# Rotary embedding of a transformer block's projection: pairs in two channel tiles, products on VectorE, sums on GpSimd

## What is computed

```python
h = rmsnorm(x, g1) * (1 + scale1) + shift1
q, k, v = split(h @ w_qkv + b_qkv, 3)          # 16 heads of 32 channels
x0, x1 = q[..., 0::2], q[..., 1::2]            # the same for k
q = interleave(x0 * cos - x1 * sin, x1 * cos + x0 * sin)
attn = softmax(q @ k.T / sqrt(32)) @ v
```

## Time and profile before

| | before |
|---|---|
| median of 3 runs | 3583.11 us (3581.57 to 3583.68) |
| the profiled execution's own time | 3584.84 us |
| its span in the trace | 3583.0 us |
| busy: PE, DVE, ACT, POOL | 90%, 57%, 44%, 46% |
| `stage_a` in the trace | about 67 us to 438 us |
| one of its blocks in the steady part | 44.27 us |
| PE busy in that block, granted clock | 38.09 us, 0.92 of full speed |
| DVE, ACT, POOL busy in that block | 35.35, 17.45, 11.46 us |

### The profile page before, as it was taken

How to read it: one execution, slowest core, us unless ns; L and a number is a source line. 1 busy time by engine, 2 the same in 40 slices (tenths; PEclk the granted TensorE clock), 3 DMA queues, 4 the chain that set the end, 5 groups by cost and what they waited for, 6 DMA issues and landing times. The chain is left out here.

```text
span 3583.0 us, 53307 instructions
## 1 busy us (share of the span) xinstructions
PE 3218.5 (90%) x15180; PEld 2074.7 (58%) x15180; DVE 2025.6 (57%) x3254; ACT 1572.8 (44%) x2848; POOL 1665.3 (46%) x732
## 2 busy tenths in 40 slices
PE   5888789999999999999999994433999998999999
PEld 5666644444444444444444442432888886788887
DVE  2887677878777876878787783533322221322222
ACT  1333217676677766777676773233211111211111
POOL 0222318888788887888788886554100000100000
PEclk9999859999999999999999997766999999999999
DMA  4444449898898988899798987554411211411210
GB/s 168 141 141 142 134 91 194 179 195 189 165 196 183 194 176 171 181 188 199 160 194 178 193 191 166 170 182 161 144 47 47 94 47 49 143 66 47 94 47 24
DMA packets 179320, 508.04 MB, mean 142 GB/s; under 512 B 25914, under 2 KB 43434, under 8 KB 145966
## 3 DMA queue, kind: packets, MB, share of 16 engines
q0 software_dynamic: 36240, 248.53, 34.2%
q1 hardware_dynamic: 132308, 233.59, 21.7%
q10 hardware_dynamic: 10512, 22.81, 1.9%
HBM read 175.18 MB, written 93.62 MB: 75 GB/s over the span
## 5 line engine op out<-in xcount | busy, mean ns | idle before, releaser
L733 DVE TENSOR_REDUCE b_mpart<-b_m 128x1 f32<-128x512 f32 x2136 | 1325.9, 685 | 385.2 <-PE b_m L783 381.3
L672 ACT ACTIVATE b_pt<-b_s 128x512 f32<-128x512 f32 x2048 | 1115.0, 596 | 522.3 <-PE b_s L808 466.4
L711 POOL TENSOR_TENSOR b_acc<-b_acc,b_pt 128x2048 f32<-128x2048 f32 x225 | 1049.2, 4663 | 204.9 <-DMA b_pt<-b_pt 204.2
L808 PE MATMUL b_s<-b_qs,b_ks 98*128 98x512 f32 x2050 | 890.9, 435 | 23.7 <-ACT b_pt L672 23.7
L783 PE MATMUL b_m<-b_ks,b_qs 96*128 96x512 f32 x2136 | 787.2, 415 | 20.5 <-issue 20.2
L808 PEld LDWEIGHTS b_s<-b_qs,b_ks 98*128 98x128 f32 x2050 | 387.3, 189 | 675.3 <-ACT b_pt L672 617.5
L860 PE MATMUL b_o<-b_pt,b_vg 128*32 128x512 f32 x4096 | 549.5, 609 | 0.0
L783 PEld LDWEIGHTS b_m<-b_ks,b_qs 96*128 96x128 f32 x2136 | 417.6, 196 | 96.2 <-DVE b_mpart L733 26.3
L1245 DVE SCALAR_TENSOR_TENSOR d_uf<-d_a,keep_chan,d_sg 128x512 f32<-128x512 f32 x128 | 96.1, 751 | 578.1 <-PE d_a L1273 578.1
L1197 POOL DMA_DIRECT2D d_raw<-in_w_fc x32 | 24.0, 755 | 591.7 <-POOLq L1122 495.7
L1216 ACT ACTIVATE d_sg<-d_g,keep_chan 128x512 f32<-128x512 f32 x128 | 88.1, 689 | 419.7 <-PE d_g L1273 419.7
(11 more groups left out here) (130 smaller groups left out, 3606.6 us busy)
## 6 DMA issues: line engine op xcount, KB each, us to landing
b_pt<-b_pt POOLq DMA_DIRECT2D x225, 1024.0 KB, 8.1
b_ks<-scratch_qk_hi SPq DMA_DIRECT2D x36, 512.0 KB, 5.6
b_qs<-scratch_qk_hi SPq DMA_DIRECT2D x68, 256.0 KB, 5.5
scratch_qk_hi<-a_q_hi SPq DMA_DIRECT2D x64, 256.0 KB, 2.5
scratch_qk_lo<-a_q_lo SPq DMA_DIRECT2D x64, 256.0 KB, 2.8
d_h_hi<-scratch_h_hi SPq DMA_DIRECT2D x16, 1024.0 KB, 7.4
d_h_lo<-scratch_h_lo SPq DMA_DIRECT2D x16, 1024.0 KB, 9.6
d_y<-scratch_y SPq DMA_DIRECT2D x16, 1024.0 KB, 8.0
```

The costliest lines, as they stand in the source:

```text
L672: act.activation(pt[:, kt % RING, h, :], ps_s[:, i % LEAD, :], ACT.Exp, scale=SCALE).then_inc(p_ready, 1)
L711: pool.tensor_tensor(acc[slot][:], acc[slot][:], pt[:, (2 * n + 3) % RING, :, :], ALU.add).then_inc(pool_added, 1)
L733: dve.tensor_reduce(mpart[slot][:, i // 4, i % 4:i % 4 + 1], ps_m[:, i % EARLY, :], AX.X, ALU.max).then_inc(max_done, 1)
L808: pe.matmul(ps_s[:, i % LEAD, :], ks[kslot][0:QR, h, kt * P:(kt + 1) * P], qs[qslot][0:QR, h, :], start=True, stop=True).then_inc(st_done, 1)
```

## The change

The host lays the channels of q and k apart: of every 256 channels the even ones come first and the odd ones second, in weights and bias. Two neighbouring channel tiles are then one pair: tile 2p holds x0 and tile 2p+1 holds x1 of the same heads. The tables of cosine and sine have the same rows for both and no sign.

- VectorE makes four products for a pair with one instruction each, `scalar_tensor_tensor`, (PSUM + bias) x table, straight from `ps_qk`: x0 cos, x0 sin, x1 sin, x1 cos.
- GpSimd makes the two sums (`rotate`: a subtraction and an addition of products) into `yq`, and one pair later the two remainders (`split_lo`).
- ScalarE keeps the rounding (`round_q`) and loses the copy out of PSUM. The norm's `squares`, `roots` and `normalise` come behind the rounding of pairs 0, 1 and 2; `means` and `rstd` on VectorE come behind the products of pairs 1 and 2.
- TensorE waits for the products of the pair two before, in place of ScalarE's copies.
- SyncE stores `hi` of pair p and then `lo` of pair p-1. Each store is again 128 rows of 2 KB; in HBM a head's 16 even channels now stand ahead of its 16 odd ones.

```diff
+        prod = m.sb("prod", [P, 2, 4, TB])
+        yq = m.sb("yq", [P, 2, 2, TB])
 # SyncE
+                for p in range(NP):
+                    store("qk_hi", q_hi, hi_ready, 0, hi_stored, it, s, p)
+                    if p:
+                        store("qk_lo", q_lo, lo_ready, 4, lo_stored, it, s, p - 1)
+                store("qk_lo", q_lo, lo_ready, 4, lo_stored, it, s, NP - 1)
 # ScalarE
-                    act.activation(q[:, t % 2, :], ps_qk[:, t % 4, :], ACT.Identity,
-                                   bias=chan[:, C_BQK + t:C_BQK + t + 1]).then_inc(q_ready, 1)
+                for p in range(NP):
+                    round_q(blk, p)
                     if more:
-                        if t == 2:
+                        if p == 0:
                             squares(blk + 1)
-                        if t == 3:
+                        if p == 1:
                             roots(blk + 1)
-                        if t == 4:
+                        if p == 2:
                             normalise(blk + 1)
 # GpSimd
+            def rotate(blk, p):
+                pair = NP * blk + p
+                pool.wait_ge(prod_ready, 4 * pair + 4 + 8)
+                pool.wait_ge(lo_ready, 2 * pair + 2)
+                for half, op in enumerate((ALU.subtract, ALU.add)):
+                    pool.tensor_tensor(yq[:, p % 2, half, :], prod[:, p % 2, 2 * half, :], prod[:, p % 2, 2 * half + 1, :], op).then_inc(yq_ready, 1)
...
             def body(it, s, more):
+                blk = 2 * it + s
+                for p in range(NP):
+                    rotate(blk, p)
+                    if p:
+                        split_lo(blk, p - 1)
+                split_lo(blk, NP - 1)
 # VectorE
-                    dve.stream_shuffle(rot[:, t % 2, :], q[:, t % 2, :], swap).then_inc(shuf_done, 1)
+                    for half, table, to in ((0, cos, 0), (0, sin, 3), (1, sin, 1), (1, cos, 2)):
+                        t = 2 * p + half
+                        dve.wait_ge(qk_ps, 2 * pair + half + 1)
+                        dve.wait_ge(yq_ready, 2 * pair + 2)
+                        dve.nop(nofuse=True)
+                        dve.scalar_tensor_tensor(prod[:, p % 2, to, :], ps_qk[:, t % 4, :], chan[:, C_BQK + t:C_BQK + t + 1],
+                                                 table[:, now], ALU.add, ALU.mult).then_inc(prod_ready, 1)
                     if more:
-                        if t == 2:
+                        if p == 1:
                             means(blk + 1)
-                        if t == 3:
+                        if p == 2:
                             rstd(blk + 1)
 # TensorE
-                    pe.wait_ge(q_ready, NT * blk + t + 1)
+                    pe.wait_ge(prod_ready, 4 * (NP * blk + t // 2) + 4)
```

More of the change, by code:

```diff
@@ L237, in _ @@
             for i in range(2):
[L238 removed]
+                sp.sem_inc(hi_stored[i], 32)
+                sp.sem_inc(lo_stored[i], 32)
                 sp.sem_inc(v_stored[i], 16)
@@ L242, in _, with store @@
             sp.dma_start(x[:], xv[1, 0]).then_inc(x_in, 16)
+            def store(name, src, ready, credit, done, it, s, p):
+                pair = NP * (2 * it + s) + p
+                for half in range(2):
+                    sp.wait_ge(ready, 2 * pair + half + 1 + credit)
+                    sp.dma_start(qk_out[name][p // 2, s, p % 2, half, :, :, bass.ds(it * TB, TB)],
+                                 f32(src[:, p % 2, half, :])).then_inc(done[p % 2], 16)
             def body(it, s, more):
                 blk = 2 * it + s
[L246 to L251, removed]
+                for p in range(NP):
[3 more added lines that the diff above has]
+                store("qk_lo", q_lo, lo_ready, 4, lo_stored, it, s, NP - 1)
                 if more and not (isinstance(it, int) and s == 0):
@@ L321, in body, with round_q @@
                         round_h(blk + 1, 1 - s, c)
[L323 to L327, removed]
+            def round_q(blk, p):
+                pair = NP * blk + p
+                for half in range(2):
+                    act.wait_ge(yq_ready, 2 * pair + half + 1 + 4)
+                    act.wait_ge(hi_stored[p % 2], 32 * (NP // 2 * blk + p // 2 + 1))
+                    act.activation(q_hi[:, p % 2, half, :], yq[:, p % 2, half, :], ACT.Copy).then_inc(hi_ready, 1)
             run(act, body)
@@ L332, in _, with split_lo @@
         def _(pool):
-            pool.sem_inc(qc_ready, 2)
-            def body(it, s, more):
[L336 to L341, removed]
+            pool.sem_inc(yq_ready, 4)
+            pool.sem_inc(lo_ready, 4)
+            def rotate(blk, p):
+                pair = NP * blk + p
+                pool.wait_ge(prod_ready, 4 * pair + 4 + 8)
+                pool.wait_ge(lo_ready, 2 * pair + 2)
+                for half, op in enumerate((ALU.subtract, ALU.add)):
+                    pool.tensor_tensor(yq[:, p % 2, half, :], prod[:, p % 2, 2 * half, :], prod[:, p % 2, 2 * half + 1, :], op).then_inc(yq_ready, 1)
+            def split_lo(blk, p):
+                pair = NP * blk + p
+                for half in range(2):
+                    pool.wait_ge(hi_ready, 2 * pair + half + 1)
+                    pool.wait_ge(lo_stored[p % 2], 32 * (NP // 2 * blk + p // 2 + 1))
+                    pool.tensor_tensor(q_lo[:, p % 2, half, :], yq[:, p % 2, half, :], f32(q_hi[:, p % 2, half, :]),
+                                       ALU.subtract).then_inc(lo_ready, 1)
+            def body(it, s, more):
+                blk = 2 * it + s
[4 more added lines that the diff above has]
+                split_lo(blk, NP - 1)
             run(pool, body)
```

66 lines of the change are left out of this document (21 added, 45 removed).

## The result

The changed kernel takes 3562.75 us (median of 5 runs, 3560.96 to 3568.23) against 3583.11 us before, 20 us less. The ratio, taken over all runs of both, is 0.9949 with a 95% interval of 0.9937 to 0.9961, which is 14 to 23 us faster. The profiled execution took 3560.96 us, with a span of 3558.8 us, 24.2 us shorter than that of before.

A forecast was written before the change was run, and what follows sets the result against it. TensorE (90% busy) was taken as the bound, its projection pauses waiting for `hf` from a late VectorE. From 3583.0 us, 27 us for seven blocks and 5 us for the last were subtracted: 3551 us, range 3531 to 3574.

The forecast's parts named there:

- a full fall of the clock in each block: Projection blocks: TensorE drops to 1.2 GHz behind every pause, costing 2.7 us each; 41.8 us a block, 3561 us in all.
- The place of the pause and the products' price: Projection: TensorE's 6.16 us wait for `hf` goes, 3.8 us on `normalise` replaces it; products take 0.75 us with GpSimd busy.
- The rival that products and GpSimd exclude each other: Projection: each product waits for one GpSimd operation (1.25 + 0.75 us), a pair costs 8 us; 3596 us, chance 0.07.
- GpSimd at 1.25 us an operation: Projection: GpSimd's 16 added operations take 20 us a block, 5.0 us a pair against TensorE's 5.6, so it keeps up.
- VectorE near 20.5 us a block: Projection: VectorE loses 26.8 us of rotation, gains 12.0 us of products, falling from 35.35 to about 20.5 us a block.
- `rstd` held up by GpSimd: Projection, behind pair 2's products: four small operations each wait for one GpSimd operation, 4 x 1.24 us; `rstd` ready at 23.6.
- the race: `rstd`'s reciprocal and GpSimd's sums start within 0.1 us; rival with all four small operations unhindered: 3528 us, chance 0.13.
- The starved `means`: Projection: `means` gets in only at 18.0 us behind four GpSimd operations, transposes start at 28.2; 3574 us, chance 0.10.
- The clock behind the pause: Projection: a 3.8 us pause lies between 2.05 (full pace) and 4.56 (slowed); 0 to 2.7 us a block, middle 1.35 taken.
- The last block: Projection's last block, without `rstd`: last v store issued at 36.2 us from its start instead of 41.3, a gain of 5 us.
- I take nothing: SyncE's q and k stores: new HBM order bounded at nothing to 0.33 us more an issue; zero taken since 2 KB rows stay whole.
- The prediction's other remark: Other projection blocks: v stores queued behind the last remainder's store cost nothing, but would from a delay of about 2 us.

The follow-up runs named there:

- the copy: Changed kernel with ScalarE copying each q/k tile with bias to SBUF and VectorE multiplying from there, not from PSUM: 3572.38 us, ratio 0.9985 to the kernel before.
- the SyncE order alone: Changed kernel with eight instructions of satisfied waits (3544.54 us), plus next input's load and first two v stores issued ahead of last pair's lo stores: 3544.83 us.
- the first edits: Against 3544.54 us (changed kernel, eight added instructions): norm one pair earlier 3541.39; also ScalarE rounding h tiles 0, 1 before pair 3 3541.15; only SyncE's store order 3544.83.
- all three together: Changed kernel with eight added instructions (3544.54 us), plus earlier norm, ScalarE's earlier rounding of h tiles 0 and 1, and SyncE's new store order: 3516.41 us.

## Why the prediction came out as it did

The forecast was 3551 with a range of 3531 to 3574; the measured 3562.75 lies inside, 12 us above it. That it lies inside is in part luck: the projection stage gained more than forecast, and a stage that the sum left out lost more than that. It is also near the number that the prediction gave for a full fall of the clock in each block (3561). That is chance too: the clock fell in four blocks, and the missing time is elsewhere.

**The place of the pause and the products' price: right.** The argument was that TensorE waits for `hf` because VectorE is 11 us behind, that the products cost 0.75 us from PSUM, GpSimd busy or not, and that the wait for `hf` goes. Measured were 0.742 us and no such wait. The rival that products and GpSimd exclude each other (3596) is refuted for the PSUM source. From SBUF they do get in each other's way, as the copy showed: 0.93 to 0.98 us a product on average and up to 1.79, though not the 2.0 for each that the rival took.

**GpSimd at 1.25 us an operation: nearly.** Sums took 1.29 us and remainders 1.34 on average, 20.6 us a block for the 20 forecast. It kept up.

**VectorE near 20.5 us a block: too low.** It was 25.0 and 24.6. The sum left out the work that now meets a busy GpSimd: four `h_lo` at 0.97 us on average instead of 0.69 (1.1 us), and the small operations of the norm, 4.9 us a block instead of 1.9. With these 4.1 us it is 24.6. The schedule had the second term, the sum of VectorE's time had not. It is not what made the total wrong: TensorE's waits in these blocks end on `normalise`.

**`rstd` held up by GpSimd: right in kind, one step too many.** The forecast had all four small operations waiting, 1.24 us each. In the steady block the race went to VectorE for the first one:

```profile
220.66 0.16 DVE L68 TENSOR_TENSOR a_newton<-a_rstd 128x4 f32<-128x4 f32 x1
220.86 1.17 DVE L70 TENSOR_TENSOR a_newton<-a_newton,a_ms 128x4 f32<-128x4 f32 x1
222.06 1.23 DVE L72 TENSOR_SCALAR a_newton<-a_newton 128x4 f32<-128x4 f32 x1
223.32 1.21 DVE L74 TENSOR_TENSOR a_rstd<-a_rstd,a_newton 128x4 f32<-128x4 f32 x1
...
227.95 1.53 DVE L384 TENSOR_SCALAR a_hf<-a_t,keep_cond_ab 128x512 f32<-128x512 f32 x2 [0.78 <-PE a_t L433]
```

The Trainium skill, page "SBUF — State Buffer", section "Who interferes with whom", has such operations wait for GpSimd's to end. Three of the four agree (1.17 to 1.23 us, against 0.16 for the one that got in ahead of GpSimd's sums, which start at 220.71). So the transposes start 25.06 us after the window's start (227.26 against 202.20) and not 26.25, the pause is 2.64 us and not 3.8. In the last preparing block all four waited, and it was 3.68. The starved `means` (3574) didn't happen: the longest of the eight took 1.17 us, one GpSimd operation.

**The clock behind the pause: right that it lies between, too dear.** The middle of 0 to 2.7 us, 1.35 a block, was taken. Blocks with the same pause went both ways. The transposes and a matmul behind them, in a block where it fell and in one where it didn't:

```profile
187.43 1.09 PE L433 MATMUL a_t<-keep_ident,a_xn 128*128 128x128 f32 x8 [2.64 <-ACT a_xn L292]
...
188.68 0.63 PE L459 MATMUL a_v<-early_w_lo,a_h_hi 128*128 128x512 f32 x1
```

```profile
227.26 1.09 PE L433 MATMUL a_t<-keep_ident,a_xn 128*128 128x128 f32 x8 [2.64 <-ACT a_xn L292]
...
228.42 0.40 PE L459 MATMUL a_v<-early_w_lo,a_h_hi 128*128 128x512 f32 x1
```

At the 1.2 GHz level eight matmuls take 0.63 us instead of 0.40; this block is 1.5 us longer (39.8 against 38.3). Four of seven did so, 0.9 us a block on average. That every block pays 2.7 us is not borne out.

The prediction took the pause's length as what decides, between 2.05 and 4.56 us. The kernel with the earlier norm speaks against that. Its third v tiles stood still for different times, and the clock stayed behind the longer pause (granted 1.00 in that block) and fell 1.5 us behind the shorter one (0.96):

```profile
268.89 0.49 PE L459 MATMUL a_v<-early_w_hi,a_h_hi 128*128 128x512 f32 x1 [2.85 <-DVE a_vsb L419]
...
345.02 0.50 PE L459 MATMUL a_v<-early_w_hi,a_h_hi 128*128 128x512 f32 x1 [2.20 <-DVE a_vsb L419]
...
346.97 0.63 PE L459 MATMUL a_v<-early_w_lo,a_h_hi 128*128 128x512 f32 x1
```

The shorter pause and the cheaper clock are worth some 10 us in the seven blocks. They became 35.3 us shorter where the sum said 27, so 2 us went the other way: TensorE's own work behind the pause takes 13.0 us (227.26 to 240.26) where the sum had 12.8, and the q and k tiles take a little more than 22.4.

**The last block: 5 us forecast, 1.2 measured.** Here the failed step is "I take nothing" for the stores' new order in HBM, with nothing to 0.33 us as the bounds. The upper bound was right for the issue (0.27 more), and it wasn't free where SyncE is the last to end. The v stores behind it landed later too, which the bound left out. With plain rows the block gained 5.1 us. The prediction's other remark, that the queue is covered in the other blocks, holds for the change (the SyncE order alone gives nothing), but only as long as `normalise` covers it.

**The attention stage: missing.** The first paragraph of the prediction took it that only the projection stage is changed, and no term stood for any other. The trace of the kernel before had ScalarE's 6 us waits on "issue", and the change takes instructions out of ScalarE's code ahead of them; the prediction weighed neither. With the loop's head moved the change takes 3544.5 us, 35 us less than the kernel before on the same chip (3579.7). This is the largest error of the sum, 16 to 18 us, and in the other direction than the projection stage's. The two partly cancel.

## What to carry to other kernels

Two-input work that GpSimd runs beside VectorE stays cheap if VectorE reads PSUM; through SBUF both pay (products 0.74 us and 0.93 to 0.98 on average, GpSimd's remainders 1.34 and 1.46). When one wait is removed, read what is due next and after it: here three were stacked one behind the other, the first edits showed 3 us or nothing each, and all three together gave 27 to 28. And an edit that changes the number of an engine's instructions ahead of a hardware loop should be timed with a few instructions more there, before its time is put down to what it does.

## What the runs showed of the hardware

- The long loop of ScalarE stands still at each restart, some 6 us with its head at place 30, 180 or 226 of 256, and 12 to 13 us at 218: 18 us for this kernel, moved by eight instructions that do nothing. A shift of 68 instructions cost about as much as the edits of the arithmetic were worth (15 and 23 us).
- A store of 128 rows of 2 KB whose target is split by head and half takes 0.60 us to issue on SyncE, and 0.33 us as plain rows; stores queued behind it land after 4.4 instead of 2.6 us.
- Behind a pause of 2.64 us and the same transposes, TensorE fell to the 1.2 GHz level in the blocks at 109, 187, 265 and 345 us (the last behind 3.68), and not at 149, 227 and 305. In the kernel with plain rows and the same pauses it fell at 226 and 304 instead of 187 and 265. What decides, the runs don't show.
